# Fetching and rounding the third FFN weight in another order at the head of an AdaLN, ternary FFN and MoE kernel

## The chip, the cores and the metric

One core of a Trainium2 chip runs the whole kernel. The metric is the device time of one execution in microseconds (us); the times given are medians of several runs. Its engines are called as in the profile: PE (TensorE), DVE (VectorE), ACT (ScalarE), POOL (GpSimd) and SP, the queue from which nearly all of the head's DMAs are issued.

## The reference

The input x has 16 sequences of 256 tokens of 512 numbers, 4096 tokens. Two layers are added to it. The first is the one the change is about:

```python
def weight_quant(w):
    scale = 1.0 / jnp.clip(jnp.mean(jnp.abs(w)), EPS, None)
    return jnp.clip(jnp.round(w * scale), -1, 1) / scale
def bitlinear(x, w):          # xn = rmsnorm(x), quantized to -128..127 per token
    ...
h = jax.nn.silu(bitlinear(x, w1)) * bitlinear(x, w2)
return bitlinear(h, w3)
```

In front of it each sequence is reduced to 8 block sums, an attention over them gives one row per sequence, which is added to the sequence's tokens, and a layer norm follows. w1 and w2 are 512 to 2048, w3 is 2048 to 512. A weight can only be rounded once the mean of its absolute values is known. The second layer, a causal convolution of 16 taps and a mixture of eight experts with two per token, isn't touched.

## The kernel before, in words

The tokens are 32 tiles of 128. **The head** (up to about 105 us) loads x, w1, w2 and w3 (4 MB each), makes the attention, and turns the weights into -1, 0, 1 in bf16. **The pipeline** (`pipeline(stage)`, steps s from -4 to 34) then runs the FFN with the tiles staggered: in step s PE makes the up products of tile s (`up(s, 0)`, `up(s, 1)`) and the down product of tile s - 2, while DVE norms tile s + 3. After it come the convolution, the routing and the experts.

Every engine runs its own list of instructions in the order in which they are written out, and waits on semaphores. So an instruction that waits holds up all that is written behind it on its engine.

**A weight's way.** A 4 MB weight is fetched in four chunks of 1 MB, w1 to `stage0`, w2 to `stage1` and w3 again to `stage0`, where chunk c may come once `ternary(0, c)` has read the first weight's. Absolute sums are made chunk by chunk, on ACT (`weight_abs`, L766, with the useless elementwise result in the tile JUNKW, 128 x 2048) or on DVE (`weight_abs`, L947). PE adds them over the partitions (`weight_total`, L1372), DVE makes the scale (`mean`, L953, four one-column instructions), and DVE rounds each chunk in two passes (`ternary`, L966): L976, float32 times scale, at most 1, to int16 in TMP; L979, at least -1, to bf16 in W12 or W3. The abbreviation ternary(w, c) is chunk c of weight w, counted from 0. PE's gate half of chunk c needs ternary(0, 2c) and (0, 2c + 1), its up half ternary(1, 2c) and (1, 2c + 1), the first down product all of w3.

**A tile's way before the FFN.** DVE: sum with the attention row (`first_sum` for tiles 0 and 1, `token_sum` on POOL for the others), `stats`, `center`, `norm`, `y_max`. ACT: `square_y` (L792). POOL: `rstd` between stats and norm (L620), then `y_scales` (L636), five small instructions that need square_y and y_max, then `y_units` (L651). DVE: `y_quant` (L1058) to int16 in Iy. ACT: `cast_y` (L801) to bf16 in Qy. SP: `turn_y` (L445), a DMA transpose to QyT.

**A tile's way in the FFN.** PE `up(n, c)` (L1418): 8 gate matmuls to the one buffer GP (L1429), then 8 up matmuls to UP[c] (L1441). It waits with the gate for `silu` of the group before, since GP is one buffer. ACT `silu(n, c)` to SG. DVE `h_mul` and `h_max`, ACT `square_h`, POOL `h_scales` (L662), DVE `h_quant`, ACT `cast_h` twice, SP `turn_h` twice, PE `down(n)` (L1445).

**SP's list at the head**: w1, x, RW and QB, a wait for the first two sums of w1 (L391), Wk and Wo, GAM and BET, w2 after the block sums, the first chunk of w3, two small transfers with TZ (the taps, L409), then a wait for PROJ on ACT, its store (L411), a wait for the taps (L412), their store (L413), a wait for PROJ's landing (L414), two loads of its rows PJ (L420), three chunks of w3 (L464), and the transposes from turn_y(0) on. `stage0` is 4 x 2048 float32 per partition.

**ACT's list at the head after the attention**: square_y(0), the sum of w3's chunk 0, square_y(1), cast_y(0), sums of chunks 1 and 2, cast_y(1), sum of chunk 3, silu(0, 0), square_y(2), cast_y(2), silu(0, 1), the squares of h for tile 0 (L860 to L873), then the pipeline's stages (L836).

Of the kernel before, what the change touches and what calls it, by code (L numbers as in the profile page):

```python
# [17 lines left out]
I16 = mybir.dt.int16  # L18
I32 = mybir.dt.int32
U32 = mybir.dt.uint32  # L20
ALU = mybir.AluOpType
ACT = mybir.ActivationFunctionType
AX = mybir.AxisListType

P = 128
# [7 lines left out]
def adaln_ffn_moe(nc, x, cond, taps, rms_w, WkT, WoT, gamma, beta, w1T, w2T, w3T, Wr, We, be, out):  # L33
# [11 lines left out]
    CH = 512  # L45
# [26 lines left out]
    with ctx:  # L72
# [15 lines left out]
        def place(name, at, shape, dt=F32):  # L88
            n = 4 if dt in (F32, F32R) else 2
            size = n  # L90
            for s in shape[1:]:
                size *= s
            assert at >= 0 and at + size // 4 <= words, (name, at, size, words)
            return nc.alloc_sbuf_tensor_at(name, list(shape), dt, offset=base + 4 * at)
# [9 lines left out]
        T = place("T", a_T + RING * D, [P, 2, NP, OB])  # L104
        BD = [place(f"BD{i}", a_T + RING * D + NI * OB + 2 * GI * NQ * OB * i, [P, 2, GI, NQ * OB]) for i in range(2)]
        stage0 = place("stage0", a_T, [P, 4, FF])
        stage1 = place("stage1", a_x, [P, 4, FF])
        assert 4 * FF <= (NT - KEEP) * D
        H = [place(f"H{i}", a_h + FF * i, [P, FF]) for i in range(2)]
# [160 lines left out]
        GP, UP = PS[:, 0:2, :], [PS[:, 2:4, :], PS[:, 4:6, :]]  # L270
        DN = bank[6]
        JUNK = bank[7]


        x_in = [sem(f"x_in{i}") for i in range(8)]
# [57 lines left out]
        def tile(n):  # L333

            return 0 <= n < NT
# [42 lines left out]
        def _(sp):  # L378
# [9 lines left out]
                load_x(i)  # L388
            sp.dma_start(RW[:], bass.AP(rms_w.tensor, 0, [[0, P], [1, D]])).then_inc(att_in, 16)
            sp.dma_start(QB[:], bass.AP(cond.tensor, D, [[0, P], [1, D]])).then_inc(att_in, 16)  # L390
            sp.wait_ge(w_abs, 2)  # L391
            sp.dma_start(WkS[:], WkT.rearrange("(k p) d -> p k d", p=P)).then_inc(att_in, 16)
            sp.dma_start(WoS[:], WoT.rearrange("(k p) d -> p k d", p=P)).then_inc(wo_in, 16)
            sp.dma_start(GAM[:], bass.AP(gamma.tensor, 0, [[0, P], [1, D]])).then_inc(norm_in, 16)
# [5 lines left out]
            def load_w3(c):  # L400
                kc = KF // 4
                sp.wait_ge(w_tern, ternary_at(0, c))
                sp.dma_start(stage0[:, :, CH * c:CH * c + CH], w3T.rearrange("(k p) d -> p k d", p=P)[:, kc * c:kc * c + kc, :]) \
                    .then_inc(w_in[0][c], 16)

            load_w3(0)
            sp.wait_ge(const, 8)
            sp.dma_start(bass.AP(z_d.tensor, TOK * ZW, [[8, ZW // 8], [1, 8]]), TZ[0:ZW // 8, 0, 0:8]).then_inc(ext_in, 16)
            sp.dma_start(TZ[:, :, OB:2 * OB], taps.rearrange("(k p) u -> p k u", p=P)).then_inc(taps_in, 16)  # L409
# [50 lines left out]

            load_pj(1)
            load_pj(2)

            for c in range(1, 4):  # L464
                load_w3(c)

            TP = 4

# [105 lines left out]
        def _(pool):  # L574
# [45 lines left out]
            def rstd(n):  # L620

                t = n % 2
                pool.wait_ge(mv_done, n + 1)
                pool.tensor_scalar(RSTD[t], MV[t][:, 1:2], RMS_EPS, None, ALU.add).then_inc(var_done, 1)
                pool.wait_ge(var_done, n + 1)
                pool.tensor_tensor(RSTD[t], RSTD[t], MHALF, ALU.pow).then_inc(rstd_done, 1)

            def scales_at(n):

                return (PA - 2) * n if n < 2 else PA * n  # L630

            def units_at(n):

                return (PA - 2) * 2 + 2 * n if n < 2 else PA * n + PA - 2

            def y_scales(n):  # L636

                t = n % 2
                pool.wait_ge(ysq_done, n + 1)
                pool.tensor_scalar(YR[t], YMS[t], RMS_EPS, None, ALU.add).then_inc(pool_a, 1)  # L640
                pool.wait_ge(pool_a, scales_at(n) + 1)
                pool.tensor_tensor(YR[t], YR[t], MHALF, ALU.pow).then_inc(pool_a, 1)
                pool.wait_ge(pool_a, scales_at(n) + 2)
                pool.wait_ge(ymax_done, n + 1)
                pool.tensor_scalar(YB[t], YM[t], YR[t], CLIP, ALU.mult, ALU.max).then_inc(pool_a, 1)
                pool.wait_ge(pool_a, scales_at(n) + 3)
                pool.tensor_tensor(YI[t], YB[t], MONE, ALU.pow).then_inc(pool_a, 1)
                pool.wait_ge(pool_a, scales_at(n) + 4)
                pool.tensor_scalar(YQ[t], YR[t], YI[t], QMAX, ALU.mult, ALU.mult).then_inc(yq_done, 1)
# [52 lines left out]
                    pool.memset(BD[s - 4][:], 0.0).then_inc(bd_zero, 1)  # L702

            rstd(0)
            rstd(1)
            y_scales(0)
            token_sum(2)
            y_scales(1)
            y_units(0)
            y_units(1)  # L710
            rstd(2)
            token_sum(3)
# [50 lines left out]
        def _(act):  # L763
            sums = [0]

            def weight_abs(w, c):  # L766

                act.wait_ge(w_in[w % 2][c], 16 * (w // 2 + 1))
                if sums[0]:
                    act.wait_ge(w_abs, sums[0])  # L770
                sums[0] += 1
                src = stage0[:, :, CH * c:CH * c + CH] if w == 2 else (stage0, stage1)[w][:, c, :].rearrange("p (k c) -> p k c", k=4)
                nc.scalar.activation(JUNKW[:].rearrange("p (k c) -> p k c", k=4), src, ACT.Abs,
                                     accum_out=WPART[:, 4 * w + c:4 * w + c + 1]).then_inc(w_abs, 1)

            weight_abs(0, 1)
# [2 lines left out]
            nc.scalar.copy(RT[:].rearrange("p k m -> p (k m)"), bank[7]).then_inc(repr_Tev, 1)  # L779
            act.wait_ge(keys_done, 1)  # L780
            nc.scalar.activation(KJ[:], bank[5], ACT.Square, accum_out=KSS).then_inc(kss_done, 1)
            act.wait_ge(soft_v, 2)
            nc.scalar.activation(EROW[:, P:2 * P], EROW[:, 0:P], ACT.Exp).then_inc(soft_e, 1)
            act.wait_ge(att_pe, 1)
# [2 lines left out]
            act.wait_ge(proj_pe, 1)  # L787
            nc.scalar.copy(PROJ[0:B, :], bank[4][0:B, :]).then_inc(proj_ev, 1)
            weight_abs(1, 2)
            weight_abs(1, 3)  # L790

            def square_y(n):  # L792
                act.wait_ge(y_done, n + 1)
# [7 lines left out]
            def cast_y(n):  # L801
                act.wait_ge(yint_done, n + 1)
                nc.scalar.copy(Qy[n % 2][:], Iy[n % 2][:]).then_inc(yqt_done, 1)
# [32 lines left out]
            def stage(s):  # L836
                if s <= 0:
                    return
                if tile(s):
                    silu(s, 0)  # L840
                if s == 1:
                    square_y(3)
                elif tile(s + 1):
                    cast_y(s + 1)
                if tile(s - 1):
                    cast_h(s - 1, 0)
                if tile(s):
                    silu(s, 1)
                if tile(s - 1):
                    cast_h(s - 1, 1)  # L850
                if tile(s):
                    square_h(s, 0)
                if tile(s + 3):
                    square_y(s + 3)
                if tile(s):
                    square_h(s, 1)
                if 0 <= s - KEEP - 4 < NQ:
                    halo(s - KEEP - 4)

            square_y(0)  # L860
            weight_abs(2, 0)
            square_y(1)
            cast_y(0)
            weight_abs(2, 1)
            weight_abs(2, 2)
            cast_y(1)
            weight_abs(2, 3)
            silu(0, 0)
            square_y(2)
            cast_y(2)  # L870
            silu(0, 1)
            square_h(0, 0)
            square_h(0, 1)  # L873
            pipeline(stage)

# [69 lines left out]
        def _(dve):  # L945
# [20 lines left out]
            def ternary(w, c):  # L966

                src = (stage1 if w == 1 else stage0)[:, :, CH * c:CH * c + CH]
                if w == 2:
                    dst = W3[:, KF // 4 * c:KF // 4 * (c + 1), :]  # L970
                else:
                    dst = W12[:, :, FF * w + CH * c:FF * w + CH * c + CH]
                rounded = TMP[:].rearrange("p (k c) -> p k c", k=4)
                if chunks[0]:
                    dve.wait_ge(w_tern, chunks[0])
                nc.vector.tensor_scalar(rounded, src, WSC[w], 1.0, ALU.mult, ALU.min).then_inc(w_round, 1)  # L976
                chunks[0] += 1
                dve.wait_ge(w_round, chunks[0])
                nc.vector.tensor_scalar(dst, rounded, -1.0, None, ALU.max).then_inc(w_tern, 1)  # L979
# [37 lines left out]
            dve.wait_ge(const, 8)  # L1017
            nc.vector.tensor_scalar(ABM[:], MSK[:, 0:1].broadcast_to([P, P]), ATC, None, ALU.mult).then_inc(att_v, 1)
            nc.vector.tensor_scalar(AMX[:], MSK[:], ATC, None, ALU.mult).then_inc(att_v, 1)
            weight_abs(1, 0)  # L1020

            def first_sum(n):

# [120 lines left out]
            stats(0)  # L1144
            center(0)
            first_sum(1)
            stats(1)
            norm(0)
            y_max(0)
            center(1)  # L1150
            norm(1)
            y_max(1)
            mean(1)
            y_quant(0)
            ternary(1, 0)
            ternary(1, 1)
            ternary(1, 2)
            y_quant(1)
            ternary(1, 3)
            stats(2)  # L1160
            center(2)
            norm(2)
            y_max(2)
            h_mul(0, 0)
            h_max(0, 0)
            y_quant(2)
            stats(3)
            center(3)
            h_mul(0, 1)
            h_max(0, 1)  # L1170
            mean(2)
            ternary(2, 0)
            ternary(2, 1)
            norm(3)
# [195 lines left out]
        def _(pe):  # L1370
# [83 lines left out]

            def stage(s):
                if tile(s):
                    if s == 1:
                        weight_total(2)
                    up(s, 0)
                    up(s, 1)  # L1460
                if s == 2:
                    pe.wait_ge(w_tern, 12)
                if s == NT + 1:
                    pe.wait_ge(xw_in[0], 16 * 2 * NQ * B // 2)
                    pe.wait_ge(halo_done, NQ)
                    pe.wait_ge(silu_done, NH * NT)
                    conv(0, 0)
                if tile(s - 2):
                    down(s - 2)
# [144 lines left out]
```

## Time and profile before

| | us |
|---|---|
| median of 3 runs | 845.53 |
| lowest, highest | 844.99, 846.36 |
| the profiled execution | 845.81 |
| its span, first to last instruction | 844.1 |
| PE busy in it | 740.7 (88%) |
| DVE, POOL, ACT busy in it | 564.4, 477.3, 396.8 |

The profile is one execution. Its times are microseconds from the start of the span. A row of a timeline gives start, duration, engine, line, operation, output and input tiles, shapes and a count (neighbouring equal instructions are merged), and in brackets the idle time before it and who ended that. L12 is line 12 of the kernel. The clock is what was granted to PE, 1.00 for 2.4 GHz and 0.50 for 1.2 GHz. For a DMA the duration on SP is that of its issue; the time to landing is counted from the start of the issue.

### The profile page before, as it was taken

Reading aid. Unit: us, or ns where it says so; the run is one execution under the profiler, and the core shown is the slowest. Engines: PE = TensorE matmul, PEld = TensorE weight load, DVE = VectorE, ACT = ScalarE, POOL = GpSimd, SP = SyncE. Lnnn points to the kernel's source line nnn. Section 1 sums busy time; section 2 is a strip of 40 time slices with the busy share of each in tenths; the row PEclk is TensorE's granted clock in tenths of the full one; section 3 lists DMA queues with packets and bytes.
Section 4 is the critical chain, followed back from the end, with each engine's and each line's share of the span. In section 5 each row is a group of like instructions: output and inputs, shape, how many; then the busy total and the mean of one; then the engine's idle time right before and its main releaser. Section 6 shows DMA issues by size and latency. Waiting matters only on the chain.

```text
span 844.1 us, 12610 instructions
## 1 busy us (share of the span) xinstructions
PE 740.7 (88%) x3913; PEld 432.6 (51%) x3945; DVE 564.4 (67%) x831; ACT 396.8 (47%) x635; POOL 477.3 (57%) x738
## 2 busy tenths in 40 slices
PE   1745599999999999999989999657999999899994
PEld 0112244444444444444446653345788888778773
DVE  2469999999999999997734424397834654444442
ACT  2056466666768877776412524034322333333332
POOL 1037889888888888884200000003567766876864
PEclk9987899999999999999999999768999999999998
DMA  9984148899999985555698999986468778877876
GB/s 359 388 328 134 31 88 149 137 182 180 178 180 189 183 157 132 117 116 92 138 232 148 113 116 258 116 197 215 77 126 165 143 136 160 152 146 143 167 143 105
DMA packets 230270, 137.50 MB, mean 163 GB/s; under 512 B 162798, under 2 KB 195054, under 8 KB 229054
## 3 DMA queue, kind: packets, MB, share of 16 engines
q1 hardware_dynamic: 210094, 99.94, 59.0%
q0 software_dynamic: 15456, 36.47, 23.2%
q10 hardware_dynamic: 4656, 0.30, 0.5%
q8 instruction: 33, 0.54, 0.3%
q14 instruction: 31, 0.25, 0.1%
HBM read 80.27 MB, written 35.42 MB: 137 GB/s over the span
## 4 chain that ended last, share of the span: by engine, by line
PE 45%; DMA 13%; POOL 11%; DVE 11%; issue 9%; SPq 6%; ACT 4%; POOLq 0%; DVEq 0%; ACTq 0%
DMA out_x<-YS,IDS 8%; PE PS L1480 8%; PE PS L1452 7%; PE PS L1572 7%; PE PS L1429 7%; PE PS L1441 7%; PE PS L1507 4%; POOL out_x L751 3%; SPq L381 2%; POOL ZR L742 2%; DVE Ih L1085 2%; PE PS L1529 1%; DMA QyT<-Qy 1%; ACT Qh L818 1%; DMA QT<-Qh 1%
## 5 line engine op out<-in xcount | busy, mean ns | idle before, releaser
L1572 PE MATMUL PS<-W,ZH 128*128 x552 | 179.5, 406 | 8.2 <-DVE ZL L1339 6.1
L742 POOL DMA_INDIRECT ZR<-z_scratch,IDG x69 | 69.6, 1008 | 156.1 <-DVE IDS L1303 135.4
L1429 PE MATMUL PS<-W,QyT 128*128 128x512 bf16 x502 | 123.0, 387 | 26.8 <-DMA QyT<-Qy 15.2
L751 POOL DMA_INDIRECT out_x<-YS,IDS x69 | 110.8, 1606 | 59.1 <-SPq L560 29.7
L939 ACT ACTIVATE YS<-YS,SG 128x512 f32<-128x512 f32 x69 | 50.0, 724 | 159.9 <-DVE YS L1357 159.9
L1441 PE MATMUL PS<-W,QyT 128*128 128x512 bf16 x504 | 120.9, 381 | 0.4
L1452 PE MATMUL PS<-W,QT 128*128 128x512 bf16 x498 | 116.4, 383 | 4.4 <-DMA QT<-Qh 2.9
L1572 PEld LDWEIGHTS PS<-W,ZH 128*128 128x128 f32 x552 | 100.4, 191 | 29.7 <-issue 11.5
L1572 PE MATMUL PS<-W,ZL 128*128 x276 | 109.6, 397 | 0.0
L1339 DVE TENSOR_TENSOR ZL<-PS,ZH 128x512 fp32r<-128x512 f32 x69 | 47.7, 691 | 78.2 <-ACT ZH L928 78.2
L1429 PEld LDWEIGHTS PS<-W,QyT 128*128 128x128 bf16 x512 | 49.7, 99 | 90.0 <-DMA QyT<-Qy 17.3
L812 ACT ACTIVATE SG<-PS,sm 128x1024 f32<-128x1024 f32 x64 | 71.0, 1109 | 45.5 <-PE PS L1429 45.5
L818 ACT CAST Qh<-Ih 128x1024 bf16<-128x1024 int16 x64 | 66.4, 1040 | 52.5 <-DVE Ih L1085 52.5
L1452 PEld LDWEIGHTS PS<-W,QT 128*128 128x128 bf16 x512 | 50.4, 99 | 65.7 <-issue 5.5
L1441 PEld LDWEIGHTS PS<-W,QyT 128*128 128x128 bf16 x512 | 50.4, 98 | 61.5 <-issue 2.1
L1071 DVE TENSOR_TENSOR H<-SG,PS 128x1024 f32<-128x1024 f32 x64 | 77.7, 1214 | 3.4 <-PE PS L1441 3.1
L1357 DVE TENSOR_TENSOR YS<-PS,BEB 128x512 f32<-128x512 f32 x69 | 47.6, 690 | 48.0 <-DMA out_x<-YS,IDS 26.0
L1077 DVE TENSOR_REDUCE sm<-H 128x1 f32<-128x1024 f32 x64 | 78.1, 1220 | 2.2
L1480 PE MATMUL PS<-XW,BD 128*64 128x128 f32 x512 | 74.2, 477 | 0.3 <-DVE BD L1135 0.3
L826 ACT ACTIVATE SG<-H 128x1024 f32<-128x1024 f32 x64 | 67.2, 1050 | 0.7 <-DVE H L1071 0.7
L1480 PEld LDWEIGHTS PS<-XW,BD 128*64 128x64 f32 x512 | 47.9, 165 | 26.4 <-issue 1.2
L1572 PEld LDWEIGHTS PS<-W,ZL 128*128 128x128 f32 x276 | 52.4, 190 | 11.7
(217 smaller groups left out, 1059.8 us busy)
## 6 DMA issues: line engine op xcount, KB each, us to landing
XW<-out_x SPq DMA_DIRECT2D x64, 240.0 KB, 4.5
X<-in_x SPq DMA_DIRECT2D x32, 256.0 KB, 10.0
out_x<-X SPq DMA_DIRECT2D x32, 256.0 KB, 3.6
z_scratch<-ZZ SPq DMA_DIRECT2D x8, 1024.0 KB, 24.1
WRAW<-in_We SPq DMA_DIRECT2D x8, 1024.0 KB, 12.6
XR<-in_x SPq DMA_DIRECT2D x20, 256.0 KB, 4.1
stage<-in_w1T SPq DMA_DIRECT2D x4, 1024.0 KB, 8.0
stage<-in_w2T SPq DMA_DIRECT2D x4, 1024.0 KB, 11.9
```

What stands on the lines that cost most here:

```text
L742: pool.indirect_dma_start(ZR[m % UZ][:], None, z_d, bass.IndirectOffsetOnAxis(IDG[:, m:m + 1].bitcast(U32), 0)) \
L751: pool.indirect_dma_start(x1_d, bass.IndirectOffsetOnAxis(IDS[:, m:m + 1].bitcast(U32), 0), YS[m % UN][:], None, compute_op=ALU.add).then_ ...
L812: nc.scalar.activation(SG[c][:], GP.rearrange("p a c -> p (a c)"), ACT.Silu, scale=OG[n % 2]).then_inc(silu_done, 1)
L818: nc.scalar.copy(Qh[:, half], Ih[:, half]).then_inc(qh_done, 1)
L826: nc.scalar.activation(SG[c][:], H[n % 2][:, half], ACT.Square, scale=FF ** -0.5, accum_out=(HSB if c else HSA)[n % 2]).then_inc(hsq_done, 1)
L1071: nc.vector.tensor_tensor(H[n % 2][:, half], SG[c][:], UP[c].rearrange("p a c -> p (a c)"), ALU.mult) \
L1077: nc.vector.tensor_reduce(HMC[n % 2][:, c:c + 1], H[n % 2][:, half], AX.X, ALU.max, apply_absolute_value=True).then_inc(hmc_done, 1)
L1429: i = nc.tensor.matmul(GP[:, a, :], QyT[t][:, k, :], W12[:, k, o:o + CH], start=(k == 0), stop=(k == KD - 1))
L1441: i = nc.tensor.matmul(UP[c][:, a, :], QyT[t][:, k, :], W12[:, k, o:o + CH], start=(k == 0), stop=(k == KD - 1))
L1452: i = nc.tensor.matmul(DN, QT[t][:, k, :], W3[:, k, :], start=(k == 0), stop=(k == KF - 1))
L1480: i = nc.tensor.matmul(PS[P // 2 * u:P // 2 * u + P // 2, b % 8, HB2 * (q % 4):HB2 * (q % 4) + HB2], BD[c % 2][:, u, q, :], XW[:, HB2 * h: ...
L1572: x = nc.tensor.matmul(bank[i], zz[i % 2][:, k, :], W2[:, bass.ds(q, 1), part, k, :].rearrange("p o d -> p (o d)"), start=(k == 0 and n == ...
```

## The change

1. **SP**: all four chunks of w3 are fetched right behind w2, ahead of the taps; the wait for two sums of w1 is gone.
2. **Sums**: ACT's elementwise waste for w1 and w2 goes to PSUM banks 0 to 3 (JUNK4), for w3 still to JUNKW. The sum of w2's chunk 0 moves from DVE to ACT, that of chunk 3 from ACT to DVE. PE's `weight_total(2)` moves from step 1 to step 0, between the two groups of tile 0.
3. **Rounding of w3**: ACT makes the first pass, float32 times scale to int16 in the place of the data (`round_w3`), DVE the second from there, with both bounds in one pass.
4. **Order**: tile 0's norm, maximum and quantization come before tile 1's stats on DVE; POOL's y_scales(0) before rstd(1), and its wait indices follow; on ACT square_y(1) and cast_y(1) come behind silu(0, 0), and silu(1, 1) comes between the third and fourth round_w3, ahead of cast_h of tile 0; on DVE mean(2) comes ahead of h_mul(0, 0).

```diff
+        S16 = place("S16", a_T, [P, 4, 2 * FF], I16)
+        JUNK4 = PS[:, 0:4, :]
@@ sync
-            sp.wait_ge(w_abs, 2)
...
-            load_w3(0)
+            for c in range(4):
+                load_w3(c)
             sp.wait_ge(const, 8)
...
             load_pj(1)
             load_pj(2)
-
-            for c in range(1, 4):
-                load_w3(c)
@@ gpsimd
             rstd(0)
+            y_scales(0)
             rstd(1)
-            y_scales(0)
+            y_units(0)
+            y_scales(1)
             token_sum(2)
-            y_scales(1)
-            y_units(0)
             y_units(1)
@@ scalar
+                dst = JUNKW[:].rearrange("p (k c) -> p k c", k=4) if w == 2 else JUNK4
...
             nc.scalar.activation(KJ[:], bank[5], ACT.Square, accum_out=KSS).then_inc(kss_done, 1)
+            weight_abs(1, 0)
...
             weight_abs(1, 2)
-            weight_abs(1, 3)
+
+            def round_w3(c):
+
+                act.wait_ge(w_step, 12)
+                act.wait_ge(w_abs, 9)
+                nc.scalar.activation(S16[:, :, 2 * CH * c:2 * CH * c + CH], stage0[:, :, CH * c:CH * c + CH], ACT.Copy, scale=WSC[2]) \
+                    .then_inc(w_round, 1)
...
                 if s == 1:
+                    round_w3(2)
+                    silu(1, 1)
+                    round_w3(3)
                     square_y(3)
...
-                if tile(s):
+                if tile(s) and s > 1:
                     silu(s, 1)
...
             square_y(0)
             weight_abs(2, 0)
-            square_y(1)
             cast_y(0)
             weight_abs(2, 1)
             weight_abs(2, 2)
-            cast_y(1)
             weight_abs(2, 3)
             silu(0, 0)
+            square_y(1)
+            cast_y(1)
+            silu(0, 1)
+            round_w3(0)
+            square_h(0, 0)
             square_y(2)
             cast_y(2)
-            silu(0, 1)
-            square_h(0, 0)
+            round_w3(1)
             square_h(0, 1)
             pipeline(stage)
@@ vector
+                if w == 2:
+                    dve.wait_ge(w_round, 8 + c + 1)
+                    nc.vector.tensor_scalar(dst, S16[:, :, 2 * CH * c:2 * CH * c + CH], 1.0, -1.0, ALU.min, ALU.max).then_inc(w_tern, 1)
+                    return
...
-            weight_abs(1, 0)
...
             first_sum(1)
-            stats(1)
             norm(0)
             y_max(0)
+            weight_abs(1, 3)
+            y_quant(0)
+            stats(1)
+            mean(1)
+            ternary(1, 0)
             center(1)
+            ternary(1, 1)
             norm(1)
             y_max(1)
-            mean(1)
-            y_quant(0)
-            ternary(1, 0)
-            ternary(1, 1)
             ternary(1, 2)
             y_quant(1)
             ternary(1, 3)
+            mean(2)
+            h_mul(0, 0)
+            h_max(0, 0)
             stats(2)
             center(2)
             norm(2)
             y_max(2)
-            h_mul(0, 0)
-            h_max(0, 0)
+            h_mul(0, 1)
+            h_max(0, 1)
             y_quant(2)
             stats(3)
             center(3)
-            h_mul(0, 1)
-            h_max(0, 1)
-            mean(2)
             ternary(2, 0)
             ternary(2, 1)
             norm(3)
@@ tensor
                 if tile(s):
-                    if s == 1:
+                    up(s, 0)
+                    if s == 0:
                         weight_total(2)
-                    up(s, 0)
                     up(s, 1)
```

## Rows read from the trace of the kernel before

**Rows 1.** Windows: us; busy PE, PEld, DVE, ACT, POOL; clock, DMA share, GB/s.
```profile
63.00:68.00 5.00, 0.00 (x0) 0.00 (x0) 4.86 (x6) 2.62 (x3) 4.64 (x5) 0.50 1.05 397
83.00:104.00 21.00, 11.94 (x46) 4.66 (x45) 20.34 (x28) 10.11 (x16) 18.38 (x24) 0.84 0.13 26
...
250.00:350.00 100.00, 99.29 (x453) 45.02 (x462) 95.00 (x115) 75.45 (x111) 85.63 (x175) 1.00 0.83 160
```

**Rows 2.** Timeline of PE: start us, us, form, count, idle before and its releaser.
```profile
71.63 3.19 PE L1429 MATMUL PS<-W,QyT 128*128 128x512 bf16 x7 [13.49 <-DMA QyT<-Qy]
...
95.13 3.57 PE L1429 MATMUL PS<-W,QyT 128*128 128x512 bf16 x8 [6.46 <-ACT SG L812]
...
103.28 1.90 PE L1429 MATMUL PS<-W,QyT 128*128 128x512 bf16 x8 [2.55 <-ACT SG L812]
```

**Rows 3.** Timeline of SP's queue, 36 to 75 us: start, us of issue.
```profile
39.78 1.44 SPq L409 DMA_DIRECT2D TZ<-in_taps  x1
...
56.55 0.99 SPq L420 DMA_DIRECT2D PJ<-proj_scratch  x2
...
64.01 7.87 SPq L450 DMA_TRANSPOSE QyT<-Qy  x2
```

**Rows 4.** DMA issues near 39.8, 57.1, 64.0 and 103.8 us: KB, us to landing.
```profile
TZ<-in_taps SPq DMA_DIRECT2D x1, 32.0 KB, 16.3
...
PJ<-proj_scratch SPq DMA_DIRECT2D x1, 256.0 KB, 4.7
...
QyT<-Qy SPq DMA_TRANSPOSE x1, 7.2
...
QyT<-Qy SPq DMA_TRANSPOSE x1, 2.4
```

**Rows 5.** Timeline of ACT, 72 to 75 us.
```profile
72.75 1.28 ACT L812 ACT_TABLE_LOAD   x1
74.86 1.11 ACT L812 ACTIVATE SG<-PS,sm 128x1024 f32<-128x1024 f32 x1 [0.82 <-PE PS L1429]
```

**Rows 6.** Groups of ACT by line, 60 to 104 us: busy us, mean ns, idle before.
```profile
L773 ACT ACTIVATE JUNKW<-stage 128x2048 bf16<-128x2048 f32 x4 | 7.6, 1907 | 2.1 <-DMA stage<-in_w3T 2.0
...
L826 ACT ACTIVATE SG<-H 128x1024 f32<-128x1024 f32 x4 | 4.2, 1054 | 0.7 <-DVE H L1071 0.7
L803 ACT CAST Qy<-Iy 128x512 bf16<-128x512 int16 x4 | 2.5, 615 | 5.2 <-DVE Iy L1063 5.2
L798 ACT ACTIVATE PS<-Y 128x512 f32<-128x512 f32 x4 | 2.4, 596 | 7.7 <-DVE Y L1048 7.7
L818 ACT CAST Qh<-Ih 128x1024 bf16<-128x1024 int16 x2 | 2.1, 1039 | 2.7 <-DVE Ih L1085 2.7
```

**Rows 7.** Windows of POOL alone: span, busy us (count), clock, DMA.
```profile
76.90:79.30 2.40, 1.92 (x5) 1.00 0.29 96
63.10:69.50 6.40, 6.00 (x6) 0.50 1.16 364
```

**Rows 8.** Groups of DVE by line, 60 to 104 us.
```profile
L976 DVE TENSOR_SCALAR TMP<-stage,sm 128x2048 int16<-128x2048 f32 x8 | 10.4, 1296 | 0.2
L979 DVE TENSOR_SCALAR W<-TMP 128x2048 bf16<-128x2048 int16 x8 | 5.6, 697 | 0.3
...
L960 DVE RECIPROCAL sm<-sm 128x1 f32<-128x1 f32 x2 | 0.3, 164 | 0.1
```

**Rows 9.** Timeline of DVE, 66 to 80 us.
```profile
68.66 0.69 DVE L979 TENSOR_SCALAR W<-TMP 128x2048 bf16<-128x2048 int16 x1
...
71.86 0.69 DVE L1033 BATCH_NORM_STATS2 sm<-Y 128x6 f32<-128x512 f32 x1
...
76.88 1.22 DVE L1071 TENSOR_TENSOR H<-SG,PS 128x1024 f32<-128x1024 f32 x1
...
79.30 0.49 DVE L1063 TENSOR_SCALAR Iy<-Y,sm 128x512 int16<-128x512 f32 x1
```

More of the change, by code:

```diff
@@ L628, in scales_at @@
             def scales_at(n):
-                return (PA - 2) * n if n < 2 else PA * n
+                return PA * n
             def units_at(n):
-                return (PA - 2) * 2 + 2 * n if n < 2 else PA * n + PA - 2
+                return PA * n + PA - 2
             def y_scales(n):
@@ L772, in weight_abs @@
                 src = stage0[:, :, CH * c:CH * c + CH] if w == 2 else (stage0, stage1)[w][:, c, :].rearrange("p (k c) -> p k c", k=4)
-                nc.scalar.activation(JUNKW[:].rearrange("p (k c) -> p k c", k=4), src, ACT.Abs,
+                dst = JUNKW[:].rearrange("p (k c) -> p k c", k=4) if w == 2 else JUNK4
+                nc.scalar.activation(dst, src, ACT.Abs,
                                      accum_out=WPART[:, 4 * w + c:4 * w + c + 1]).then_inc(w_abs, 1)
```

## The prediction

> **What bounds the kernel now.** I read the windows first. In the long middle of the FFN stage TensorE is busy 99.3 of 100 us at full clock; from 83 to 104 us it is busy 11.9 of 21 while VectorE is busy 20.3 [rows 1]. So the middle is TensorE's own work, nothing there can hide or return a shift, and only the head has time to give. Then TensorE's timeline: the first FFN matmul waits 13.49 us for QyT and starts at 71.63; the second tile pair stops 6.46 us at 95.13 and 2.55 us at 103.28, both for an SG of ScalarE. The group at 103.28 is the gate half of tile 2, second chunk, G(2,1) below; after it TensorE runs through [rows 2]. **The forecast is therefore one number: when G(2,1) starts.** What it moves by, the end moves by. The profiled execution took 845.81 us for a span of 844.1, 0.3 above the median of 845.53; I add the shift to the median.
>
> **Where the first transpose stands.** SP is one queue in program order. Its transpose of tile 0 is issued at 64.01 and lands 7.2 us later, at 71.2, call that T; alone a transpose takes 2.4 [rows 3, 4]. The 4.8 us between are the three 1 MB fetches of w3 in front of it, issued from 57.6, right after PJ's loads. The other row to see: the 32 KB load of the taps is issued at 39.78 and takes 16.3 us, to 56.1, because the second weight and the first w3 chunk are in front of it [rows 3, 4]. What SP issues lands in the order of issue, whatever its size.
>
> **The change on SP.** The three chunks go right behind the first, ahead of the taps. At 397 GB/s [rows 1] 1.049 MB is 2.64 us, three are 7.9. The chunks follow chunk 0, which the taps row puts just under 56.1: they land at about 58.7, 61.3 and 63.9, and the taps at 56.1 + 7.9 = 64.0. But SP waits for the taps, then for PROJ's store, then issues the two PJ loads (0.99 us, before from 56.55), and only then the transpose. PJ at 64.4, transpose at 65.4. So the new T is at least 65.4 + 2.4 = 67.8; at most 65.4 + 4.7 = 70.1, what the second PJ load took in a filled queue [rows 4]. PJ's half megabyte is directly in front, so I take 69.1. The transpose gains 2.1 us. What tile 0's new place in VectorE's and POOL's order gains for its input is more, but is covered by SP's wait for the taps.
>
> **What rests on T then.** The edit in ScalarE's order decides. Before, square_y(1) ran before the w3 sums. Now it stands behind silu(0,0), which waits for the first gate group, which waits for T. Counting from T, where a pass that follows another directly overlaps it by 0.05 to 0.1:
> - silu(0,0) starts at 74.86 = T + 3.65 and ends T + 4.8 [rows 5].
> - square_y(1) 0.60 and its accumulator: T + 5.5. y_scales(1) on POOL 2.4: T + 7.9 [rows 6, 7]. Nothing else of POOL's is in the way.
> - y_quant(1) 0.5, then ternary(1,3) 1.30 + 0.70 on VectorE: T + 10.35 [rows 8]. VectorE has had nothing since ternary(1,2), which ends near 69.4 as it does now [rows 9]: it stands idle until 77.0, **7.6 us**. That is the new wait. Queued behind it are the last quarter of w2 (for the up half of chunk 1) and all of tiles 0 and 2.
> - mean(2) four times 0.16: T + 10.95; h_mul and h_max(0,0) 2.42: 13.35; stats to y_max of tile 2, 5.02: 18.4; h_mul and h_max(0,1) 2.42: 20.8; y_quant(2) 0.5: T + 21.3 [rows 8, 9].
> - ScalarE: cast_y(2) 0.55, round_w3(1) 1.85, square_h(0,1) 1.05: silu(1,0) starts T + 24.75, ends 25.85, at 95.0 [rows 6].
> - TensorE: U(0,1) waits for ternary(1,3), T + 10.35 to 12.3; QyT(1) is there at T + 11.6 (cast 0.6, transpose 2.4 [rows 4, 6]), so the two groups of up(1,0) end near T + 15.9, and then it stands 10 us. After 6.46 us idle the clock was low and eight matmuls took 3.57, after 2.55 they took 1.90 [rows 2]. I take the low one: G(1,1) ends and silu(1,1) starts at T + 29.3.
> - Then ScalarE without a pause: silu(1,1) 1.0, round_w3(3) 1.85, square_y(3) 0.6, two cast_h 1.9, square_h(1,0) 1.05, square_y(4) 0.6, square_h(1,1) 1.05, silu(2,0) 1.1 from T + 37.35 [rows 5, 6]. G(2,1) starts as it ends: **T + 38.5**.
>
> A round is priced as the 1.91 us Abs of the same 128x2048 tile [rows 6], less overlap; no row has ScalarE writing int16 in place. Bounds: 1.0, if 16-bit output halved it, to 3.8, twice the row; two of the four (chunks 1 and 3) are on the path, chunk 2 is under the slow G(1,1). I take the row. The remaining VectorE half is int16 to bf16 like the 0.70 pass now.
>
> **Sum.** 69.1 + 38.5 = 107.6 against 103.28: +4.3 us, 849.8 us. The savings are real but covered: VectorE loses four rounds, 4 x 1.30 = 5.2 us [rows 8], but waits 7.6. Its own chain stays a little under ScalarE's: h_scales(0), six small POOL steps like the five in 2.4 us, ends T + 27.7 (an estimate); h_quant(0) 1.3, h_mul and h_max(1,0) 2.4, two passes 1.4, norm(4) 0.7, h_mul(1,1) 1.2: T + 34.7; with square_h and silu G(2,1) would start at T + 37 [rows 7 to 9]. At nothing I cost: sums written to PSUM (banks 0 to 3 are unused until T), the removed wait of SP on two sums (SP is then still issuing X loads), weight_total(2) one stage earlier (it is one small product between two groups), the sums exchanged between the engines (the last w2 sum runs on VectorE while POOL makes tile 0's scales). Were their cover gone, each would cost its own instruction, 2 us at most.
>
> POOL's 2.4 has a second price in the trace: 6.4 us for tile 1's scales while rounds of w2 ran on VectorE [rows 7]. I take 2.4, since VectorE stands idle there. The Trainium skill's page "SBUF — State Buffer", section "Who interferes with whom", says that a VectorE pass using two ports and a GpSimd instruction exclude each other for a whole instruction; by that rule the idle VectorE gives 2.4, and the two values are its two cases.
>
> **Rivals.**
> 1. *T lands early, no change.* If small transfers overtook big ones, SP's waits would pass near 56 and the transpose would be free. Then ScalarE decides: the last chunk lands at 63.9, the sums (1.91 each and their accumulators) end about 66.6, table load 1.28 [rows 5] and silu(0,0) end at 69.0, as if T were 64.2. G(2,1) at 102.7: -0.6, 844.9. Against it stands the taps row. The Trainium skill's page "DMA: Bandwidth & Descriptors", section "Queues, rings and completion order", says that completion is not first-in first-out per issuing engine, though each DMA engine takes descriptors in ring order; the first half would give this case, the second mine. 14%.
> 2. *Faster: VectorE's work alone sets the end.* It is busy 20.3 of 21 us, and 5.2 us leave it. With T at 64.2 its wait at y_quant(1) is 64.2 + 7.9 - 69.4 = 2.7, and 5.2 - 2.7 = 2.5 are won: 843.0. The point is a T under 66.9, and ScalarE's rounds must find gaps. 10%.
> 3. *Slower still.* y_scales(1) at 6.4 instead of 2.4, or rounds at 3.8: +4.0 on top, 853.8. For it: only the one slow row. 10%.
> 4. *The fetches aren't earlier at all* (SP's queue holds them back): then the w3 sums come late too; within the forecast's numbers, not counted apart.
>
> The forecast has 66%: with T from 67.8 to 70.1 alone +3.0 to +5.3, with the clock high for G(1,1) 1.7 less, so 847.0 to 851.5. **Range** 844.5 to 852.5, which takes in rival 1 and leaves out 2 and 3. A measurement of this kernel tells 0.2%, 1.7 us, from no change. Faster 10%, same 14% (rival 1), slower 76% (forecast, rival 3).
>
> **What will show it.** First QyT landing near 69; the taps landing near 64; an idle of VectorE of some 7 us before the second Iy, released by POOL; silu(1,0) at 94 or later; ScalarE nearly full from there to silu(2,0); G(2,1) near 107.6. An idle under 5 us at that Iy, or a QyT under 66.9, would make it wrong, as would TensorE gaps in the middle that differ from now.

## The result, and the profile after

| | before | changed |
|---|---|---|
| median of 5 runs, us | 845.53 | 852.76 |
| lowest, highest | 844.88, 846.77 | 850.81, 854.21 |
| profiled execution; its span | 845.81; 844.1 | 852.82; 851.0 |

The ratio is 1.0079 with a 95% interval of 1.006 to 1.0098: 7.2 us slower, where 4.3 were forecast. The sign and the mechanism came as forecast; the size is 2.9 us over the forecast and a quarter of a microsecond past the upper end of the range.

First the windows of the changed kernel, as in [rows 1] (us; busy PE, PEld, DVE, ACT, POOL; clock, DMA share, GB/s):

```profile
83.00:104.00 21.00, 10.81 (x44) 4.59 (x44) 18.90 (x24) 12.93 (x13) 13.17 (x23) 0.76 0.07 20
250.00:350.00 100.00, 99.53 (x457) 45.27 (x464) 95.60 (x115) 75.49 (x112) 86.03 (x172) 1.00 0.88 165
```

The middle is as full as it was. In the head VectorE has become emptier (18.9 of 21 us for 20.3) and so have POOL (13.2 for 18.4) and TensorE (10.8 for 11.9), while ScalarE has gone from 10.1 to 12.9. Work was taken from VectorE, the fullest engine there, and VectorE now waits.

TensorE's timeline; the last row is G(2,1), after which it runs through:

```profile
71.54 3.19 PE L1445 MATMUL PS<-W,QyT 128*128 128x512 bf16 x7 [12.88 <-DMA QyT<-Qy]
...
82.37 1.90 PE L1457 MATMUL PS<-W,QyT 128*128 128x512 bf16 x8 [2.83 <-DVE W L995]
...
97.91 3.19 PE L1445 MATMUL PS<-W,QyT 128*128 128x512 bf16 x7 [10.19 <-ACT SG L819]
...
110.39 2.84 PE L1445 MATMUL PS<-W,QyT 128*128 128x512 bf16 x8 [4.11 <-ACT SG L819]
```

Against [rows 2] the first group starts as before (71.54 for 71.63), and G(2,1) 7.1 us later (110.39 for 103.28). The head's loss is made between these two rows. Between them stand a new wait of 2.83 us for VectorE's last quarter of w2, and one of 10.19 in front of G(1,1), for silu(1,0). The longest wait of before, 6.46 us, stood one group later, in front of G(2,0), for silu(1,1).

SP's queue, and then the time to landing of what it issued at 54.99 and 66.86 and of the fourth chunk, whose issue begins at about 40.8:

```profile
38.64 13.61 SPq L404 DMA_DIRECT2D stage<-in_w3T  x4
52.29 2.65 SPq L410 DMA_DIRECT2D z_scratch<-TZ  x1
54.99 0.39 SPq L411 DMA_DIRECT2D TZ<-in_taps  x1
55.42 2.67 SPq L413 DMA_DIRECT2D proj_scratch<-PROJ  x1
65.41 0.38 SPq L415 DMA_DIRECT2D taps_scratch<-TZ  x1
65.83 0.99 SPq L422 DMA_DIRECT2D PJ<-proj_scratch  x2
66.86 15.40 SPq L452 DMA_TRANSPOSE QyT<-Qy  x2
```

```profile
TZ<-in_taps SPq DMA_DIRECT2D x1, 32.0 KB, 10.4
...
QyT<-Qy SPq DMA_TRANSPOSE x1, 4.2
...
stage<-in_w3T SPq DMA_DIRECT2D x1, 1024.0 KB, 24.3
```

The four chunks took SP 13.6 us to issue, not four times 0.45: with w2's four chunks and w3's first three in front, the issue itself stood until about 52. The taps were issued at 54.99 in place of 39.78. They landed at 65.4, right behind the fourth chunk (40.8 + 24.3 = 65.1), and the transpose followed at 66.86 and landed at T = 71.1. Before, T was 71.2.

VectorE, with idle times and who ended them; four of ScalarE's silu (L819: silu(0,0), (1,0), (1,1) and (2,0)) with the square (L805) and a rounding pass (L796); then POOL's sum beside the second Iy:

```profile
67.32 0.69 DVE L995 TENSOR_SCALAR W<-TMP 128x2048 bf16<-128x2048 int16 x1
78.92 1.47 DVE L1078 TENSOR_SCALAR Iy<-Y,sm 128x512 int16<-128x512 f32 x1 [10.90 <-POOL sm L648]
```

```profile
74.77 1.11 ACT L819 ACTIVATE SG<-PS,sm 128x1024 f32<-128x1024 f32 x1 [6.36 <-PE PS L1445]
75.78 0.59 ACT L805 ACTIVATE PS<-Y 128x512 f32<-128x512 f32 x1
...
96.36 1.09 ACT L819 ACTIVATE SG<-PS,sm 128x1024 f32<-128x1024 f32 x1
97.36 1.99 ACT L796 ACTIVATE S<-stage,sm 128x2048 int16<-128x2048 f32 x1
101.14 1.11 ACT L819 ACTIVATE SG<-PS,sm 128x1024 f32<-128x1024 f32 x1 [1.79 <-PE PS L1445]
...
109.24 1.10 ACT L819 ACTIVATE SG<-PS,sm 128x1024 f32<-128x1024 f32 x1
```

```profile
78.84 1.26 POOL L617 TENSOR_TENSOR Y<-X,PJ 128x512 f32<-128x512 f32 x1
```

The main loss stands in two rows: VectorE ends ternary(1,2) at 68.0 and begins its next instruction at 78.92. The square of tile 1 could have run at 65.4, when its norm was done (65.37), and ran at 75.78, directly behind silu(0,0). The row names POOL, but POOL's y_scales(1) had itself stood until that square.

### The profile page after: what moved, and what is told of

Read it like the earlier page. It is cut to its first block, busy times and chain, and to the rows that moved or that the text cites. A ratio compares the mean times of both kernels' runs of the same rounds, so it can differ in the third digit from the quotient of the medians.

```text
span 851.0 us, 12613 instructions
## 1 busy us (share of the span) xinstructions
PE 742.2 (87%) x3913; PEld 432.9 (51%) x3945; DVE 561.3 (66%) x827; ACT 404.9 (48%) x639; POOL 470.9 (55%) x738
## 4 chain that ended last, share of the span: by engine, by line
PE 42%; POOL 10%; issue 10%; DMA 9%; DVE 7%; SPq 4%; ACT 3%; POOLq 0%; DVEq 0%; ACTq 0%
PE PS L1496 8%; PE PS L1445 8%; PE PS L1468 7%; PE PS L1457 7%; DMA out_x<-YS,IDS 6%; PE PS L1588 4%; PE PS L1523 4%; POOL out_x L750 3%; POOL ZR L741 2%; DMA QyT<-Qy 2%; PE PS L1545 1%; DVE AOH L1299 1%; ACT ZH L940 1%; SPq L460 1%; ACT Qh L825 1%
## 5 line engine op out<-in xcount | busy, mean ns | idle before, releaser
L819 ACT ACTIVATE SG<-PS,sm 128x1024 f32<-128x1024 f32 x64 | 71.1, 1111 | 53.0 <-PE PS L1445 52.6
```

Source lines behind the costliest of these rows:

```text
L819: nc.scalar.activation(SG[c][:], GP.rearrange("p a c -> p (a c)"), ACT.Silu, scale=OG[n % 2]).then_inc(silu_done, 1)
```

## The experiments

The names: **A**, the order on ScalarE costs; **B**, only the late transpose costs; **C**, ScalarE's added rounding passes cost. All ratios are to the kernel before on the same chip; the chips differ by up to 1.7% (the kernel before took 859.8, 859.5 and 848.1 us in the three sets), so times are compared through their ratios alone. "Changed" is the changed kernel. Starts of G(2,1) are read from one profiled execution each; the changed kernel's was 110.39 on one chip and 110.30 on another (e9).

**e1, the square put back early** (in "changed"):

```diff
             weight_abs(2, 2)
+            square_y(1)
             weight_abs(2, 3)
+            cast_y(1)
             silu(0, 0)
-            square_y(1)
-            cast_y(1)
```

> The changed kernel with square_y(1) put back ahead of the last w3 sum and cast_y(1) ahead of silu(0,0). Theory A (the order on ScalarE is what costs: VectorE idles 10.9 us at the second Iy because tile 1's square stands behind silu(0,0)): that idle falls under 3 us, G(2,1) starts some 4 to 6 us earlier, near 105, and the time falls from 852.8 to about 847. Theory B (the late transpose of tile 0 alone costs, the order doesn't): the time stays within 1 us of 852.8, since QyT of tile 0 still lands near 71.

Measured 1.0000 (0.9975 to 1.0024). The idle at the second Iy is 1.88 us and G(2,1) starts at 105.48, 4.9 earlier than in the changed kernel, while the first group is within about 0.5 us of where it was. B is refuted: by the trace 4.9 of the 7.1 us go with two lines. By the ratio all of the loss goes, but its interval is 2 us wide to each side, so the two agree.

```profile
71.03 3.60 PE L1445 MATMUL PS<-W,QyT 128*128 128x512 bf16 x8 [11.19 <-DMA QyT<-Qy]
...
105.48 2.33 PE L1445 MATMUL PS<-W,QyT 128*128 128x512 bf16 x8 [3.86 <-ACT SG L819]
```

**e2, tile 0's transpose first** (in "changed"; the pipeline's own turn_y(0) is left out):

```diff
             sp.dma_start(proj_d, PROJ[0:B, :]).then_inc(proj_out, 16)
+            sp.wait_ge(yqt_done, 1)
+            sp.dma_start_transpose(QyT[0][:], Qy[0][:]).then_inc(qyt_in[0], 16)
             sp.wait_ge(taps_in, 16)
```

> The changed kernel with tile 0's transpose issued ahead of SP's waits for the taps and for PROJ's landing, and of the PJ loads. Theory A: the transpose lands near 66 in place of 71, held only by the last w3 chunk (65.1) in front of it; silu(0,0) starts near 68.5 to 69.7 and the whole chain behind it moves with it, so G(2,1) starts near 105 and the time is about 847.5. Theory B expects the same here, 847 to 848. Rival C (ScalarE's rounds set the rhythm of the head whatever comes first): at most 2 us are won, over 850.5.

Measured 1.0004 (0.9978 to 1.003). The transpose is issued at 59.40 and lands after 6.4, at 65.8; G(2,1) starts at 105.12. So the other half of the mechanism holds too: T moves 5.3 us and the chain behind it 5.3. C's bound (at most 2 us won) fails. A stands; this run alone can't tell A from B, e1 does.

**e3, both.**

> Both edits of the two runs before. If the two waits are in series (A), their gains add until VectorE's own work is the chain: with VectorE never idle from 60 us its work, 5.2 us less than in the kernel before, lets G(2,1) start near 100, and the time is about 842 to 843. If ScalarE is the bound then (C), it stays at or over 845.5.

Measured 0.9986 (0.996 to 1.0012), no measurable gain over before, and a miss: G(2,1) starts at 102.04, not near 100, and the ratio is 844.3 us on the first chip's scale, not 842 to 843. Of the 4.9 and 5.3 us, 10.2 together, 8.4 come. What is next in the way is seen at the gate group of tile 1's second chunk:

```profile
89.15 3.59 PE L1447 MATMUL PS<-W,QyT 128*128 128x512 bf16 x8 [7.59 <-ACT SG L821]
...
102.04 3.60 PE L1447 MATMUL PS<-W,QyT 128*128 128x512 bf16 x8 [3.61 <-ACT SG L821]
```

It waits 7.59 us for silu(1,0), whose input was there from 79.8; ScalarE's list puts square_y(2), cast_y(2), a rounding pass and square_h(0,1) in front. So C is right in this much: once the two waits are shorter, ScalarE's list is in the way.

**e4, the fetch undone** (in "changed": chunks 1 to 3 again behind the PJ loads).

> The changed kernel with only the fetch undone: chunks 1 to 3 of w3 are issued behind the PJ loads again, as in the kernel before. My theory: the early fetch gains nothing, since the transpose waits for the same 3 MB either way, first in the queue of transfers (before) and now in SP's waits; the transpose lands at 70.5 to 71.3 and the time is within 1 us of 852.8. Rival: the early fetch does give back something, through the w3 sums that end at 67 in place of 73: then this is 2 us or more slower than the changed kernel.

Measured 1.0077 (1.0048 to 1.0106). The first group starts at 71.60, G(2,1) at 110.87. In this order the early fetch gives at most 0.5 us by the trace, and nothing that the ratios can tell: ScalarE's sums end at 67 or at 73, and silu(0,0) starts only near 75 in either. With the transpose first, silu(0,0) starts at 69.7 (e6), and no run has the late fetch there; what the early fetch gives in e6 is open.

**e5, w3 rounded by VectorE again** (in "changed": round_w3 is left out of ScalarE's list, `ternary(2, c)` has its two passes).

> The changed kernel with w3 rounded by VectorE in both passes again, ScalarE's four passes gone, all else as changed. My reckoning says that both engines' chains end within 2 us of each other, so moving the pass gives ScalarE 7.6 us back and costs VectorE 5.2: VectorE becomes the chain, G(2,1) starts some 2 to 3 us later than in the changed kernel (110.4), and the ratio to the kernel before is 1.010 to 1.012 where the changed kernel had 1.008. Rival C (ScalarE's rounds are what costs): the ratio falls to 1.004 or less.

Measured 1.0122 (1.0081 to 1.0163); G(2,1) starts at 113.61, 3.2 us later than in the changed kernel. C as a cause of the loss is refuted: it asked for 1.004 or less. Handing the passes to ScalarE helps by the trace, as the reckoning of both chains said, though the ratio's interval overlaps the changed kernel's (1.0079, and 1.0103 in e9); it helps less than it takes off VectorE (5.2 us), since ScalarE's chain ends close behind.

**e7, one part of the change alone, in the kernel before**: ScalarE's square_y(1) and cast_y(1) behind silu(0,0), with POOL's y_units(0) ahead of y_scales(1).

> The kernel before with one part of the change alone: square_y(1) and cast_y(1) behind silu(0,0) on ScalarE, with POOL's y_units(0) ahead of y_scales(1) so that it can run. Theory A: VectorE idles some 10 us at the second Iy (from 69 to 79), as in the changed kernel, and with all four rounding passes still on VectorE the ratio is 1.008 to 1.013. Theory B (the order costs nothing by itself): within 0.2% of 1.

Measured 1.0102 (1.006 to 1.0143), and the idle is made anew:

```profile
79.29 0.49 DVE L1063 TENSOR_SCALAR Iy<-Y,sm 128x512 int16<-128x512 f32 x1 [10.21 <-POOL sm L649]
```

G(2,1) starts at 112.73. This order, without any other part of the change, costs as much as the whole change within the intervals. A is shown from both sides.

**e8, the taps ahead of chunks 1 to 3** (in "changed").

> The changed kernel with the taps and the small store issued ahead of w3's chunks 1 to 3. If transfers of one queue land in the order of issue, the taps land near 56 in place of 65.4, but PROJ's store, still issued behind the 3 MB, lands near 65 and holds SP as long: the transpose of tile 0 gains under 1 us, and the ratio stays 1.006 to 1.009. If the taps alone held SP, the transpose lands near 63 to 66 and the ratio falls to about 1.000.

Measured 1.0064 (1.0039 to 1.009). SP's queue, and the landings of the taps and of PROJ's store:

```profile
39.77 1.52 SPq L410 DMA_DIRECT2D TZ<-in_taps  x1
41.33 13.32 SPq L404 DMA_DIRECT2D stage<-in_w3T  x3
54.70 1.82 SPq L414 DMA_DIRECT2D proj_scratch<-PROJ  x1
...
65.52 1.05 SPq L423 DMA_DIRECT2D PJ<-proj_scratch  x2
```

```profile
TZ<-in_taps SPq DMA_DIRECT2D x1, 32.0 KB, 17.6
proj_scratch<-PROJ SPq DMA_DIRECT2D x1, 32.0 KB, 10.8
```

The taps land at 57.4, but 32 KB of PROJ, behind the 3 MB, take 10.8 us to 65.5 and hold SP as long; the first group starts at 70.32, 1.2 us earlier than changed, a little more than the 1 us expected.

**e6, ScalarE's list by who waits** (e3, with silu(0,0) ahead of cast_y(1) and the silu of tile 1 moved forward; the diff is against "changed", and e2's lines and the condition that leaves silu(1, 0) out of the pipeline aren't shown):

```diff
+            square_y(1)
             weight_abs(2, 3)
             silu(0, 0)
-            square_y(1)
             cast_y(1)
             silu(0, 1)
             round_w3(0)
             square_h(0, 0)
+            silu(1, 0)
             square_y(2)
...
                 if s == 1:
-                    round_w3(2)
                     silu(1, 1)
+                    round_w3(2)
                     round_w3(3)
```

> The run with both edits (transpose first, square_y(1) early), and two more moves on ScalarE: silu(0,0) ahead of cast_y(1), and silu(1,0) ahead of square_y(2) and of the second rounding pass, silu(1,1) ahead of the third. There the wait of the gate matmuls of tile 1, second chunk, for silu(1,0) was 7.6 us. If that wait was on the chain, G(2,1) starts 2 to 4 us earlier than its 102.0 and the ratio to the kernel before is 0.994 to 0.997. If VectorE's list is the chain, these moves give at most the 1.5 us by which silu(0,0) comes earlier: 0.997 to 0.9985.

Measured 0.9959 (0.9931 to 0.9987): faster than the kernel before, about 3.5 us. G(2,1) starts at 100.41. The 7.59 us wait is gone:

```profile
79.16 1.90 PE L1448 MATMUL PS<-W,QyT 128*128 128x512 bf16 x8 [0.18 <-ACT SG L821]
...
100.41 2.72 PE L1448 MATMUL PS<-W,QyT 128*128 128x512 bf16 x8 [2.84 <-ACT SG L821]
```

But of its 7.4 us only 1.6 reach G(2,1): VectorE is the chain now, as it was before the change. From the second Iy at 70.0 to 99.8 it is busy 27.5 of 29.8 us (before: 31.3 of 33.2, from 69.5 to 102.7), with no wait over 0.62, and the last square_h ahead of silu(2,0) waits for VectorE's product, as it did before.

**e9, the changed kernel again**, and **e10**, e6 with POOL's token_sum(2) behind y_units(1), on one chip.

> The changed kernel itself, on the chip of the two runs beside it. Every theory expects the ratio that it had, 1.006 to 1.010, and G(2,1) within 1 us of 110.4.

> The run with ScalarE's new order (ratio 0.996) with POOL's token_sum(2) behind y_units(1), so that it no longer runs beside VectorE's y_quant(1), which takes 1.47 us beside it and 0.48 without. VectorE's list is the chain there by now, so G(2,1) starts about 1 us earlier than its 100.4 and the ratio is 0.9935 to 0.9965. If POOL's small steps, now beside the rounding pass of w2, take longer and hold stats(2), nothing is won.

e9: 1.0103 (1.0083 to 1.0124), just over the 1.010 expected, G(2,1) at 110.30. So the same change cost 7.2 us on one chip and, on the first chip's scale, 8.7 on another. e10: 0.9972 (0.9955 to 0.9989), over the 0.9965 expected, 845.25 against 848.10 us, G(2,1) at 99.76, and the second Iy takes 0.48 us:

```profile
70.34 0.48 DVE L1081 TENSOR_SCALAR Iy<-Y,sm 128x512 int16<-128x512 f32 x1 [1.87 <-POOL sm L650]
```

By the trace e10's G(2,1) is 0.65 us ahead of e6's, by the ratios e10 is a little behind; the intervals overlap, so whether the last move gives anything stays open. Both are faster than both kernels.

## Why the prediction was right, and where its size was off

**What held.** The loss is made ahead of G(2,1), at the wait that was named, and the savings of VectorE are real and covered. The rule that the end moves by what G(2,1) moves came out well, 7.1 us there and 6.9 in the span, but in part by luck. These are the first and the last group of down products of TensorE's unbroken run, before and then after:

```profile
106.74 3.62 PE L1452 MATMUL PS<-W,QT 128*128 128x512 bf16 x15
410.66 3.62 PE L1452 MATMUL PS<-W,QT 128*128 128x512 bf16 x15
```

```profile
115.54 3.62 PE L1468 MATMUL PS<-W,QT 128*128 128x512 bf16 x15
419.27 3.62 PE L1468 MATMUL PS<-W,QT 128*128 128x512 bf16 x15
```

The shift is 8.8 us at the first, since G(2,1) and its up half ran slower as well (told below), and 8.6 at the last, and 1.7 of it come back behind the FFN. Why they do isn't shown.

Counted from T, the chain was forecast step by step, and the trace of the changed kernel has, with T = 71.1:

| step | forecast | measured |
|---|---|---|
| silu(0,0) ends | T + 4.8 | T + 4.8 |
| POOL's y_scales(1) ends | T + 7.9 | T + 7.8 |
| y_quant(1) ends | T + 8.4 | T + 9.3 |
| silu(1,0) starts | T + 24.75 | T + 25.3 |
| silu(1,1) starts | T + 29.3 | T + 30.0 |
| silu(2,0) starts | T + 37.35 | T + 38.1 |
| G(2,1) starts | T + 38.5 | T + 39.3 |

**The term that was mis-sized is T**: 69.1 forecast, 71.1 measured, past the upper bound of 70.1. The taps landed 1.4 us after my 64.0, and the transpose took 4.2 us where I had 3.7. That is 2.0 of the 2.9 us. I had also priced the fetches' issue at nothing, but nothing shows that the 13.6 us for which SP stood issuing them made T late: the taps were issued by 55.4 and landed 10 us after that. In e5 the issue takes as long, and the fourth chunk (issued from 41.0) lands at 63.9, as forecast. The DMA rows show something else. Here are a queue's row of the changed kernel for 61 to 65.5 us (packets, MB, share of 16 engines), a window of the changed kernel (clock, DMA share and GB/s last), and the same window of e5 with e5's fourth chunk:

```profile
q8 instruction: 1, 0.02, 1.6%
```

```profile
63.70:64.60 0.90, 0.00 (x0) 0.00 (x0) 0.86 (x2) 0.00 (x0) 0.32 (x1) 0.50 0.07 23
```

```profile
63.70:64.60 0.90, 0.00 (x0) 0.00 (x0) 0.90 (x2) 0.81 (x3) 0.90 (x1) 0.50 0.05 4
stage<-in_w3T SPq DMA_DIRECT2D x1, 1024.0 KB, 22.9
```

From 63.7 to 64.6 the chunk's data come at 23 GB/s, with a share of 0.07, about one of 16 DMA engines: the others are done and one is behind. A single packet of another queue, for instructions, moved just before; its 1.6% of 16 engines over 4.5 us are, by an estimate from this row, 1.15 us on one engine, the size of the delay. In e5 it moves from 63.0 on, and there the chunk is on time and the taps behind it land at 65.1. That the packet stood on the engine that was late is likely but not shown, since the trace doesn't name the engines.

That the landing follows the order of issue was right for the head: e4 and e8 show it, and rival 1 (small transfers overtake) has the 10.8 us of PROJ's 32 KB against it. The prediction put it as a rule for all that SP issues, and that is too wide. In the kernel before, the load of PJ is issued at 131.74 and lands at 136.7, and the load of XW behind it, issued at 132.40, lands at 136.5:

```profile
PJ<-proj_scratch SPq DMA_DIRECT2D x1, 256.0 KB, 5.0
XW<-out_x SPq DMA_DIRECT2D x1, 240.0 KB, 4.1
```

The Trainium skill's page "DMA: Bandwidth & Descriptors", in "Queues, rings and completion order", has both halves: each DMA engine takes descriptors in ring order, and completion is not first-in first-out per issuing engine. The head agrees with the first, these two loads, 0.2 us out of order, with the second.

**Another 0.8 us** lies between T and G(2,1). It begins with y_quant(1), 1.47 us in place of 0.49: 0.9 at that step, of which about 0.5 are left at silu(1,0); the other 0.3 come behind silu(1,0), most of it while the slow G(1,1) ran. Beside y_quant(1) POOL ran token_sum(2), which I had placed behind y_scales(1) without asking what runs beside it on VectorE; e10 has it back at 0.48. The Trainium skill's "SBUF — State Buffer", in "Who interferes with whom", states this exclusion for both sides; the trace agrees, and I had applied it to POOL's side alone.

**The idle of VectorE** was 10.9 us, not 7.6: 2.0 are T's, and 1.4 are that ternary(1,2) ended at 68.0, not at 69.4. The 1.4 didn't move the end.

**What is left lies within the spread.** (The forecast's own band ended at 851.5, 0.7 above what its terms give, 845.5 + 5.3; the measured time is past both.) In the profiled execution G(2,1) and its up half took 2.84 and 2.68 us behind an idle of 4.11; in e9, the same kernel, G(2,1) took 1.90 behind 3.71. The rows of e9, then the window of G(2,1) in the changed kernel and in e9 (the clock is third from the end):

```profile
110.30 1.90 PE L1445 MATMUL PS<-W,QyT 128*128 128x512 bf16 x8 [3.71 <-ACT SG L819]
112.04 1.89 PE L1457 MATMUL PS<-W,QyT 128*128 128x512 bf16 x8
```

```profile
110.39:113.03 2.64, 2.64 (x9) 1.02 (x10) 2.20 (x4) 0.46 (x1) 2.31 (x5) 0.65 0.25 50
```

```profile
110.30:112.04 1.74, 1.74 (x8) 0.79 (x9) 1.60 (x4) 0.46 (x1) 1.48 (x5) 1.00 0.02 5
```

From G(2,1) to the first down product are 5.15 us in the one and 3.47 in the other. So 1.7 us hang on the granted clock, a mean of 0.65 (partly at the lower level) against 1.00, and that differs between executions of one kernel. The forecast had this group at the high clock.

Rival 2 (VectorE's work alone sets the end) had its own test: with T at 65.8 in e2 the idle was still 5.66 us and the time that of before. For the kernel as it was changed it was wrong. Its condition, VectorE's work setting the end, was met only after ScalarE's list was put in order as well, in e6, at 842.1 us on the first chip's scale (845.53 x 0.9959), near its 843.0. Rival 3 (POOL slow) didn't occur.

## What to carry to other kernels

Where an engine's list is fixed, ask of each small instruction what stands behind it on other engines, not what it costs: a 0.6 us square moved behind a silu held the fullest engine for 10.9 us, more than the 5.2 us of work that the change took off it. A fetch moved earlier in a queue moves later everything issued behind it, small transfers too, and with them the waits for those. Putting the taps alone in front of the bulk gave 1.2 us here (e8); issuing the transpose ahead of the waits that it didn't need gave 5.3 (e2). When two chains end close together, each must be mended before a saving shows: e1 and e2 moved G(2,1) by 4.9 and 5.3 us, both together by 8.4, and a gain over before that is clear of the noise came only with the third edit.

## What the runs showed of the hardware that I had not expected

Issuing isn't free once much is under way: with four chunks of w2 in front, four more 1 MB fetches held SP's queue for 13.6 us. Of the small ones behind, the two stores took 2.65 and 2.67 us to issue (L410 and L413 in the rows above) where they took 0.52 and 0.32 before, and the load of the taps between them 0.39. No run shows a cost of that hold: what was issued behind it landed 7 us or more after it. One packet of the instruction queue may have cost more, about 1.1 us on the transfers that SP waited for. A VectorE pass of 0.48 us takes 1.47 when POOL's 128x512 sum started first. And the clock behind an idle of TensorE of about 4 us is open: 3.71 us left it high in e9, 4.11 brought a slower group in the profiled execution, 3.61 a fully slow one (3.60 us) in e3.
